# Reordering block 0's attention, one block's mask, a residual sum and the last block in a hand-ordered four-layer kernel on one Trainium2 core

## The chip, the cores and the metric

The kernel runs on one core of a Trainium2 chip. The metric is device microseconds of one execution. The engines have their own instruction queues and work in order, each by itself: TensorE (PE) multiplies, VectorE (DVE), ScalarE (ACT) and GpSimd (POOL) do the elementwise work, SyncE (SP) issues most DMAs. They meet only through semaphores.

## The reference, cut to what matters

Four layers, each added to its input, on x of 128 rows x 32 tokens x 128 features. The third and the fourth choose weights by row.

```python
def _L0_cond_ref(hidden, W1, b1, v, prompt_type_ids):      # pooling with a per-row mask
    scores = jnp.einsum('bsa,a->bs', jnp.tanh(jnp.einsum('bsd,da->bsa', hidden, W1) + b1), v)
    p = jax.nn.softmax(jnp.where(mask, scores[:, None, :], NEG_INF), axis=-1)
    return jnp.einsum('bjl,bld->bjd', p, hidden) / cnt[..., None]
...
def _L1_cond_ref(...):                                     # attention, 16 heads of 8
    dense_out = jnp.einsum('bhqk,bhkd->bhqd', jax.nn.softmax(scores + bias, axis=-1), V)
    ...
    return out @ Wo.T + bo
def _L2_cond_ref(...):                                     # 512 hidden units, low-rank experts
    hidden_i = jnp.einsum('bsd,fd->bsf', x, wi)
    hidden_i += ALPHA * jnp.einsum('bsr,fr->bsf', jnp.einsum('bsd,rd->bsr', x, common_wi_a), common_wi_b)
    hidden_i = jax.nn.relu(hidden_i + _expert_lora(x, expert_ids, experts_wi_a, experts_wi_b))
    ...                                                    # the same pattern with wo, back to 128
def _L3_cond_ref(...):                                     # 512 units, 32 of 128 outputs by expert
    h = jax.nn.gelu(jnp.einsum('bnd,hd->bnh', x, fc1_w) + fc1_b, approximate=False)
    shared = jnp.einsum('bnh,sh->bns', h, fc2_w) + fc2_b
    expert_x = jnp.einsum('bnh,bph->bnp', h, experts_w[indices]) + experts_b[indices][:, None, :]
x = x + _L0_cond_ref(...); x = x + _L1_cond_ref(...); x = x + _L2_cond_ref(...); x = x + _L3_cond_ref(...)
```

## The kernel before

The 4096 tokens are cut into 8 blocks (`NBLK`) of 512 tokens, 16 rows each. Features lie on partitions. There is no scheduler: each engine's program is written out by hand, and what stands in it first runs first. Each engine has three parts.

**Preparation and block 0.** Weights are folded while they arrive. The second projection of layer 2 is folded per expert: `base_out` and `pairs_out` (PE, L821, L834) build it in four PSUM banks for each half, and `expert_out` (ACT, L528) copies it to `weff`. In between runs block 0's attention, in four groups of heads: `scores` (PE, L714), `score_max` (DVE, L1161, L1166), `subtract_max` (POOL, L382), `exps` (ACT, L507), `turn` (DVE, L1172), `weigh` (PE, L729), `normalise` (DVE, L1178, L1181). `pool_weights` (DVE, L1117 to L1136) with `l0_exps` and `spread_weights` (ACT) is the first layer's softmax for the next block. `weight_lows` (POOL, L419) and `weight_highs` (ACT) split weights into two parts. `keep_busy` (PE, L643) multiplies into a bank that nobody reads.

**Steps 1 to 7** (`step_of(n, last)`; 2 to 6 are a loop). A step holds attention of block n, layer 2 of block n-1, the second half of layer 3 of block n-2 (`last`), and pooling of block n+1. `low` and `mask_low` make the low-rank input of `hidden_expert`; `hidden` and `hidden_expert` fill a bank (list `HID`), `relu` empties it; `out_rows` (PE, L786) multiplies by the row's own weights `rwo`. Those weights are gathered from `weff`: SP copies 12 of a block's 16 rows by DMA (`gather`, L277; `DMA_ROWS`), POOL 4 (`out_weights`, L413). At the end of a step `out_turn` (PE, L793) turns layer 2's output, `x3` (DVE, L1215, L1216, L1219) adds it and splits the sum into a high part, the sum and a low part; `x2` (DVE, L1191) is the attention's sum for block n, which ACT's `x2_high` (L534) and DVE's `x2_low` (L1195) split; `fc1` (PE, L846 to L850 and one chunk more) needs the high part of x3 for its first six matmuls and then the low part; the next step's `low` (PE, L739 to L743) needs both parts of x2.

**The end.** After step 7 come layer 2 of block 7, `final` of block 6 (PE, L869), and layer 3 of block 7. POOL's `expert_weights` (L403) writes block 7's expert weights over block 6's, 4 rows as soon as one part of `final` of block 6 has read them (`row_ps`), and then `biased_x3` (L390); PE's `token_major(7)` (L859) waits for that sum, and `final_by_chunk` (L887) for all 16 rows.

Of the kernel before, what the change touches and what calls it, by code (L numbers as in the profile page):

```python
# [25 lines left out]
P = 128  # L26
# [3 lines left out]
Q4 = P // S  # L30
# [37 lines left out]
EARLY = W_END + R_END + I_END  # L68
DMA_ROWS = [r for r in range(ROWS) if r % Q4 != Q4 - 1]


def cond_resid_kernel(nc, xt, xn, ints, bools, cols, attn_w, rank_w, ffn_w, fc2t, e3t, out):
    with ExitStack() as ctx:
# [100 lines left out]
        pS = [pS0, pS1]  # L174
        GIN = [pB1, pB2, pS0, pS1]
# [62 lines left out]
        def _(sp):  # L238
# [32 lines left out]
            def gather(i):  # L271

                for r in DMA_ROWS:
# [9 lines left out]
            gather(0)  # L283
# [15 lines left out]
        def _(pool):  # L299
# [115 lines left out]

            def weight_lows(to, first, width, n):

                at(pool, w_high, n)
                pool.tensor_tensor(ffn_p[1][:, to:to + width], ffn_s[:, first:first + width],  # L419
                                   ffn_p[0][:, to:to + width], ALU.subtract).then_inc(w_low, 1)  # L420
# [10 lines left out]
                               emask[:, :].unsqueeze(2).to_broadcast([P, 2, D]), ALU.mult).then_inc(bpair_sb, 1)  # L431
            later_ids()
            weight_lows(N_EIA, W_EIA, P + F, 1)
            subtract_max(0, 2)
            weight_lows(N_FC1, W_FC1, F, 2)
            subtract_max(0, 3)
            weight_lows(N_I, W_I, F, 3)

            def step_of(n):
# [9 lines left out]
                subtract_max(n, 1)  # L449
                expert_weights(n - 1, 0)  # L450
# [17 lines left out]
        def _(act):  # L468
# [40 lines left out]
            def relu(i, c):  # L509
                at(act, hid_ps, FC * i + c + 1)  # L510
                act.activation(hid[:, c, :], [pB1, pB2, pB0, pB1][c][:, :], ACT.Relu).then_inc(hid_sb, 1)  # L511
# [61 lines left out]
            exps(0, 0)  # L573
            weight_highs(N_FC1, W_FC1, F)
            exps(0, 1)
            out_factor()
            tanh(1)
            exps(0, 2)
            l0_exps(1)
            expert_out(0, 0)  # L580
            expert_out(0, 1)
            exps(0, 3)
            expert_out(0, 2)
            expert_out(0, 3)
            spread_weights(1)
            act.wait_ge(prep, P_PRODUCTS)
            weight_highs(N_I, W_I, F)
# [39 lines left out]
            for c in range(FC):  # L627
                relu(NBLK - 1, c)
# [9 lines left out]
        def _(pe):  # L638
# [115 lines left out]
            HID = [pB1, pB2, pB0, pB1]  # L754
# [6 lines left out]
            def hidden(i, c):  # L761

                if c == 1:
# [6 lines left out]
                parts3(HID[c][:, :], weight(N_I, c), whole(x2p), True, False)  # L770

            def hidden_expert(i, c):

                at(pe, low_sb, 2 * (i + 1))
                parts3(HID[c][:, :], weight(N_EIB, c), whole(lowp), False, True, (lowl_sb, i + 1)).then_inc(hid_ps, 1)
# [153 lines left out]
            keep_busy(3, pS0, x2p[0])  # L929
# [16 lines left out]
            base_out(0, 2)
            base_out(0, 3)
            pairs_out(0)
            weigh(0, 1)
            base_out(1, 0)  # L950
            base_out(1, 1)
            weigh(0, 2)
# [8 lines left out]
            def step_of(n, last, next_block=True):  # L961
# [31 lines left out]
                hidden_expert(n - 1, 0)  # L993
                scores(n, 1)
                hidden(n - 1, 1)
# [22 lines left out]
            low(NBLK - 1)  # L1018
            final(NBLK - 2, 0, pA0)
            final(NBLK - 2, 1, pA0)  # L1020
            for c in range(FC):
                hidden(NBLK - 1, c)
                hidden_expert(NBLK - 1, c)
            final(NBLK - 2, 2, pA0)
            out_rows(NBLK - 1, *range(G))
# [10 lines left out]
        def _(dve):  # L1036
# [176 lines left out]
            def x3(i):  # L1213
                at(dve, outT_ps, i + 1)
                tt(x3p[0][:, :], pB0[:, :], x2T[:, :], ALU.add).then_inc(x3h_sb, 1)  # L1215
                tt(x3T[:, :], pB0[:, :], x2T[:, :], ALU.add).then_inc(x3_sb, 1)  # L1216
                at(dve, x3_sb, i + 1)
# [44 lines left out]
            pool_weights(1, 0)  # L1262
            turn(0, 2)
            normalise(0, 0)
# [145 lines left out]
```

## Time and profile before

| | us |
|---|---|
| median of 3 runs (lowest, highest) | 259.78 (258.68, 262.64) |
| the profiled execution's own time | 258.46 |
| its span from first to last instruction | 256.7 |
| PE busy | 245.5 (96%) |
| DVE, ACT, POOL busy | 187.5, 137.7, 121.7 |

The span is what the trace covers; 1.8 us lie around it. A busy PE says nothing on where a single stage waits, so the stages are read one by one: 0 to 39.3 us is the preparation with block 0, 39.3 to 67.1 step 1, then six steps to 231 us, and the end to 256.7.

### The profile page before, as it was taken

How to read it: one execution, taken by the hardware profiler on the slowest of the kernel's cores; microseconds unless marked ns; L12 is line 12 of the kernel's file. 1: busy time of each engine (PE TensorE's matmuls, PEld its weight loads, DVE VectorE, ACT ScalarE, POOL GpSimd, SP SyncE). 2: the span in 40 equal slices, each digit the busy share in tenths (PEclk: the TensorE clock that was granted, in tenths of full speed). 3: DMA queues.
4: the chain of work that ended last, by engine and by line, in shares of the span. 5: the costliest groups of instructions: out<-in, count | busy, mean ns of one | idle time of the engine just before them, and what ended most of it. 6: DMA issues, size and time to landing. Idle time of an engine off the chain costs nothing.

```text
span 256.7 us, 12675 instructions
## 1 busy us (share of the span) xinstructions
PE 245.5 (96%) x4862; PEld 183.9 (72%) x4862; DVE 187.5 (73%) x349; ACT 137.7 (54%) x253; POOL 121.7 (47%) x242
## 2 busy tenths in 40 slices
PE   7999999897999999999999999999999999889993
PEld 5666455676687858787778767786878587758983
DVE  4879887886878787887888787878787868563041
ACT  3175455672819653774648382858196528541250
POOL 5876612653515461645345443536154445464240
PEclk9999999999999999999999999999999999999999
DMA  6978403550455225530654055503554541255011
GB/s 182 369 238 244 137 3 125 222 208 31 127 206 208 86 76 213 204 123 6 239 204 163 0 200 200 214 0 132 200 205 189 211 169 43 84 222 193 3 43 43
DMA packets 27326, 38.27 MB, mean 149 GB/s; under 512 B 10769, under 2 KB 11537, under 8 KB 27170
## 3 DMA queue, kind: packets, MB, share of 16 engines
q1 hardware_dynamic: 26578, 36.99, 40.3%
q10 hardware_dynamic: 720, 0.89, 1.2%
q8 instruction: 20, 0.33, 0.5%
q14 instruction: 8, 0.07, 0.1%
HBM read 10.60 MB, written 2.10 MB: 49 GB/s over the span
## 4 chain that ended last, share of the span: by engine, by line
PE 82%; SPq 5%; DVE 5%; DMA 3%; ACT 2%; issue 2%; ACTq 0%; DVEq 0%
PE pB L786 11%; PE pB L869 9%; PE pB L739 7%; PE pB L743 6%; PE pooled L714 6%; PE pB L740 6%; PE pooled L682 5%; PE pV L729 4%; PE pooled L676 3%; PE pV L694 3%; SPq L277 2%; PE pV L735 2%; SPq L276 2%; PE pB L846 2%; PE pB L821 2%
## 5 line engine op out<-in xcount | busy, mean ns | idle before, releaser
L403 POOL COPY rw<-e3t_s 128x128 f32 x128 | 40.5, 317 | 54.6 <-issue 50.0
L382 POOL TENSOR_TENSOR sc<-sc,rmax 128x512 f32<-128x512 f32 x32 | 33.7, 1052 | 42.5 <-DVE rmax L1166 42.4
L507 ACT ACTIVATE ex<-sc 128x512 f32<-128x512 f32 x32 | 20.2, 630 | 27.3 <-POOL sc L382 26.9
L786 PE MATMUL pB<-rwo,hid 128*32 128x128 f32 x1024 | 33.3, 275 | 1.4 <-DMA rwo<-weff 1.3
L786 PEld LDWEIGHTS pB<-rwo,hid 128*32 128x32 f32 x1024 | 26.7, 109 | 5.1 <-issue 2.6
L1161 DVE SCALAR_TENSOR_TENSOR sc<-pooled,bias 128x512 f32<-128x512 f32 x32 | 21.7, 678 | 11.6 <-PE pooled L714 9.7
L413 POOL COPY rwo<-weff 128x512 f32 x32 | 21.4, 674 | 16.9 <-ACT weff L528 5.8
L1172 DVE STREAM_TRANSPOSE pt<-ex 128x512 f32<-128x512 f32 x32 | 22.4, 700 | 6.5 <-ACT ex L507 6.5
L511 ACT ACTIVATE hid<-pB 128x512 f32<-128x512 f32 x32 | 18.3, 594 | 12.0 <-PE pB L743 11.7
L869 PE MATMUL pB<-rw,hT 128*32 128x128 f32 x768 | 24.4, 274 | 0.0
L1166 DVE TENSOR_REDUCE rmax<-sc 128x16 f32<-128x512 f32 x32 | 22.0, 686 | 1.1
L500 ACT ACTIVATE vb<-pV 32x512 f32<-32x512 f32 x32 | 20.1, 627 | 4.0 <-PE pV L694 3.4
L869 PEld LDWEIGHTS pB<-rw,hT 128*32 128x32 f32 x768 | 20.3, 110 | 2.0 <-issue 1.4
L534 ACT ACTIVATE x_h<-x2T 128x512 fp32r<-128x512 f32 x8 | 5.1, 633 | 28.0 <-DVE x2T L1191 28.0
L1151 DVE SCALAR_TENSOR_TENSOR kb<-pooled,bqk,cols_s 128x2048 f32<-128x2048 f32 x8 | 18.7, 2343 | 1.8 <-PE pooled L682 1.8
L714 PE MATMUL pooled<-kb,qT 32*32 32x128 f32 x1024 | 18.4, 272 | 1.4 <-DVE sc L1161 1.3
L1215 DVE TENSOR_TENSOR x_h<-pB,x2T 128x512 fp32r<-128x512 f32 x8 | 5.5, 692 | 18.6 <-PE pB L793 18.6
L714 PEld LDWEIGHTS pooled<-kb,qT 32*32 32x32 f32 x1024 | 14.2, 103 | 6.1 <-issue 6.1
L739 PE MATMUL pB<-x_h,ffn_h 128*128 128x512 f32 x40 | 18.3, 457 | 0.0
L743 PE MATMUL pB<-x_l,ffn_h 128*128 128x512 f32 x40 | 16.5, 413 | 0.5 <-DVE x_l L1195 0.5
L539 ACT ACT_TABLE_LOAD x13 | 16.7, 1283 | 0.2
L729 PEld LDWEIGHTS pV<-vb,pt 128*32 128x32 f32 x1024 | 12.4, 110 | 5.0 <-issue 2.7
(181 smaller groups left out, 521.1 us busy)
## 6 DMA issues: line engine op xcount, KB each, us to landing
rwo<-weff SPq DMA_DIRECT2D x96, 256.0 KB, 2.3
rw<-fc2t_dram SPq DMA_DIRECT2D x4, 768.0 KB, 12.3
xT<-xt_dram SPq DMA_DIRECT2D x7, 256.0 KB, 2.7
xN<-xn_dram SPq DMA_DIRECT2D x7, 256.0 KB, 2.9
out_dram<-o_s SPq DMA_DIRECT2D x7, 256.0 KB, 2.3
e3t_s<-e3t_dram SPq DMA_DIRECT2D x1, 1024.0 KB, 10.5
rwo<-ffn_w_dram SPq DMA_DIRECT2D x1, 896.0 KB, 6.4
rwo<-ffn_w_dram SPq DMA_DIRECT2D x1, 512.0 KB, 12.0
```

Of the source, the lines that this page charges most:

```text
L382: pool.tensor_tensor(sc[:, g % 2, :, :], sc[:, g % 2, :, :], rmax[:, g % 2, :].unsqueeze(2).to_broadcast([P, H, S]), ALU.subtract).then_in ...
L403: pool.tensor_copy(rw[:, r, :, SHARED:D], e3t_s[:, bass.ds(e, 1), :, :].rearrange("p o c n -> p (o c) n"))\
L413: pool.tensor_copy(rwo[:, row, :, :].rearrange("p c d -> p (c d)"), weff[:, bass.ds(e, 1), :, :].rearrange("p o c d -> p (o c d)")).then_i ...
L714: last[u] = mm(by_head(pS[u])[S * q:S * q + S, :, g, :], qT[k, row], kb[k, :, row], start=True, stop=True)
L729: last = mm(pV[S * h4:S * h4 + S, at_col:at_col + w], pt[:, hg % 2, G * h4 + g, :], vb[:, g, H4 * hg + h4, :, :], start=True, stop=True)
L739: mm(ps, w[0], x[0], start=start, stop=False)
L743: return mm(ps, w[0], x[1], start=False, stop=stop)
L786: last = mm(pB2[S * q:S * q + S, P * g:P * g + P], hid[:, c, tok], rwo[:, Q4 * g + q, c, :], start=(c == 0), stop=(c == FC - 1))
L869: last = mm(ps[S * q:S * q + S, P * g:P * g + P], hT[:, c, tok], rw[:, Q4 * g + q, c, :], start=(c == 0), stop=(c == FC - 1))
L1161: stt(sc[:, g % 2, :, :].rearrange("p (h g) t -> p h (g t)", h=H4), pS[g % 2][:, :].rearrange("p (h t) -> p h t", h=H4), SCALE, bias[:, ba ...
L1166: dve.tensor_reduce(rmax[:, g % 2, :], sc[:, g % 2, :, :], AX.X, ALU.max).then_inc(mx_sb, 1)
L1172: dve.transpose(pt[:, g % 2, :, :], ex[:, g % 2, :, :]).then_inc(pt_sb, 1)
```

## The change

Five edits, all but two of them pure order.

- **Block 0.** PE: three `keep_busy` fewer before the first scores, three more taken out later (13 become 7 in this part); the next block's `scorer_in` and `weigh` come earlier, `weigh(0, 1)` and `weigh(0, 2)` ahead of `pairs_out(0)` and of `base_out(1, ...)`. ACT: `exps` ahead of `expert_out` and weight copies. POOL: `subtract_max(0, 2)` and `(0, 3)` ahead of index and weight work. DVE: `pool_weights(1, 0)` behind `turn(0, 2)` and `normalise(0, 0)`.
- **Step 1.** DVE's `mask_low(0)` stands behind both `score_max(1, 0)` and `(1, 1)`; PE's `hidden_expert(0, 0)` behind `scores(1, 1)`.
- **One row more by POOL.** Row 14 of block 0 (`POOL_ROW`) is copied by POOL behind `subtract_max(1, 1)`; SP gathers 11 rows for that block.
- **x2 sooner.** In every step `x2` stands between the first two and the last operation of `x3`.
- **Other end.** `hidden(7, 1)` fills another bank (`HID_END`) and stands ahead of `final` of block 6; `final(6, 2)` and `final(6, 3)` stand behind `out_rows(7)` and `out_turn(7)`; two `keep_busy` are gone.

```diff
+POOL_ROW = ROWS - 2
+        HID_END = [pB1, pA1, pB0, pB1]
 # SP
-            gather(0)
+            gather(0, [r for r in DMA_ROWS if r != POOL_ROW])
 # POOL
+            def one_more_row(i):
+                e = pool.value_load(e2i[0:1, bass.ds(ROWS * i + POOL_ROW, 1)], min_val=0, max_val=E2 - 1)
+                pool.tensor_copy(rwo[:, POOL_ROW, :, :].rearrange("p c d -> p (c d)"),
+                                 weff[:, bass.ds(e, 1), :, :].rearrange("p o c d -> p (o c d)"))\
+                    .then_inc(rwo_sb[POOL_ROW // Q4], 16)
+            subtract_max(0, 2)
+            weight_lows(N_EIA, W_EIA, P + F, 1)
+            subtract_max(0, 3)
             later_ids()
-            weight_lows(N_EIA, W_EIA, P + F, 1)
-            subtract_max(0, 2)
             weight_lows(N_FC1, W_FC1, F, 2)
-            subtract_max(0, 3)
 # DVE, a step
-                x3(n - 1)
+                x3_high(n - 1)
                 x2(n)
+                x3_low(n - 1)
 # DVE, x2
                 at(dve, wo_ps, i + 1)
+                at(dve, x3_sb, i)
 # PE, the end
             low(NBLK - 1)
+            hidden(NBLK - 1, 1, HID_END)
             final(NBLK - 2, 0, pA0)
             final(NBLK - 2, 1, pA0)
...
-            final(NBLK - 2, 2, pA0)
             out_rows(NBLK - 1, *range(G))
+            final(NBLK - 2, 2, pA0)
+            out_turn(NBLK - 1)
             final(NBLK - 2, 3, pA0)
-            out_turn(NBLK - 1)
             token_major(NBLK - 2, pA1)
-            keep_busy(2, pS0, ffn_p[0])
             fc1(NBLK - 1)
```

DVE in the preparation, from the third group's turn on. `pt` is `turn`, `rc` and `on` are `normalise`, `l0s` and `l0m` are `pool_weights(1, 0)`. Before:

```order
L1117 SCALAR_TENSOR_TENSOR l0s<-masked,pooled 128x128
L1120 TENSOR_REDUCE l0m<-l0s 128x4
L1122 TENSOR_TENSOR l0s<-l0s,l0m 128x128
L1172 STREAM_TRANSPOSE pt<-ex 128x512
L1178 RECIPROCAL rc<-pV 128x32
L1181 TENSOR_TENSOR on<-pV,rc 128x16x8 x2
```

The same place after:

```order
L1191 STREAM_TRANSPOSE pt<-ex 128x512
L1197 RECIPROCAL rc<-pV 128x32
L1200 TENSOR_TENSOR on<-pV,rc 128x16x8 x2
L1136 SCALAR_TENSOR_TENSOR l0s<-masked,pooled 128x128
L1139 TENSOR_REDUCE l0m<-l0s 128x4
L1141 TENSOR_TENSOR l0s<-l0s,l0m 128x128
```

The three `pool_weights` operations now stand behind the turn and a normalisation, which waits for PE's second `weigh`.

PE at the end, from the last expert chunk of layer 2 on: `pB2<-rwo,hid` is `out_rows(7)`, `pooled<-rw,hT` is `final` of block 6, `pB0<-cols_s,lowm` is `out_turn(7)`, `pooled<-cols_s,x3bn` is `token_major(6)`. Before:

```order
L869 MATMUL pooled<-rw,hT 32x128 x16
L786 MATMUL pB2<-rwo,hid 32x128 x64
L869 MATMUL pooled<-rw,hT 32x128 x16
L793 MATMUL pB0<-cols_s,lowm 128x128 x4
L859 MATMUL pooled<-cols_s,x3bn 128x128 x4
L643 MATMUL pooled<-ffn_h 128x512 x2
```

The same place after:

```order
L797 MATMUL pB2<-rwo,hid 32x128 x64
L880 MATMUL pooled<-rw,hT 32x128 x16
L804 MATMUL pB0<-cols_s,lowm 128x128 x4
L880 MATMUL pooled<-rw,hT 32x128 x16
L870 MATMUL pooled<-cols_s,x3bn 128x128 x4
```

Both parts of `final` moved back, one behind `out_rows(7)`, one behind `out_turn(7)`.

## Rows read from the trace of the kernel before

**Rows 1.** The chain that ended last, share of the span by engine.

```profile
PE 82%; SPq 5%; DVE 5%; DMA 3%; ACT 2%; issue 2%; ACTq 0%; DVEq 0%
```

**Rows 2.** Stretches: us, busy us of PE, PEld, DVE, ACT, POOL; granted clock; DMA.

```profile
12.00:39.30 27.30, 26.51 (x374) 15.61 (x370) 23.38 (x47) 15.48 (x28) 15.04 (x22) 1.00 0.53 157
39.30:67.10 27.80, 25.02 (x470) 18.54 (x467) 21.31 (x41) 15.45 (x31) 13.23 (x26) 1.00 0.38 135
94.40:121.60 27.20, 27.20 (x592) 20.94 (x591) 22.11 (x41) 16.37 (x32) 12.78 (x26) 1.00 0.38 145
```

**Rows 3.** Timeline of DVE, tail of step 2: start, us, instruction.

```profile
91.28 0.69 DVE L1219 TENSOR_TENSOR x_l<-x3T,x_h 128x512 fp32r<-128x512 f32 x1
91.89 0.74 DVE L1191 SCALAR_TENSOR_TENSOR x2T<-pV,bo_eff,x1T 128x512 f32<-128x512 f32 x1
```

**Rows 4.** Timeline of PE, the same tail.

```profile
92.19 0.63 PE L850 MATMUL pB<-x_l,ffn_h 128*128 128x512 f32 x2
...
94.08 0.50 PE L743 MATMUL pB<-x_l,ffn_h 128*128 128x512 f32 x1
94.42 1.88 PE L682 MATMUL pooled<-x1T,attn_s 128*128 128x512 f32 x4
```

**Rows 5.** Timeline of PE, the end; in brackets idle before and releaser.

```profile
230.01 0.50 PE L743 MATMUL pB<-x_l,ffn_h 128*128 128x512 f32 x1 [0.48 <-DVE x_l L1195]
231.06 1.96 PE L869 MATMUL pooled<-rw,hT 128*32 128x128 f32 x64 [0.55 <-ACT hT L515]
...
238.65 1.08 PE L869 MATMUL pooled<-rw,hT 128*32 128x128 f32 x32
239.54 3.68 PE L786 MATMUL pB<-rwo,hid 128*32 128x128 f32 x128
...
248.34 0.60 PE L859 MATMUL pB<-cols_s,x3bn 128*128 128x128 f32 x4
```

**Rows 6.** Timeline of ACT (last relu) and of POOL, the end.

```profile
238.75 0.60 ACT L511 ACTIVATE hid<-pB 128x512 f32<-128x512 f32 x1 [0.76 <-PE pB L743]
...
240.48 0.30 POOL L403 COPY rw<-e3t_s 128x128 f32 x1 [1.82 <-PE pooled L869]
241.15 0.30 POOL L403 COPY rw<-e3t_s 128x128 f32 x1 [0.37 <-issue]
...
244.85 0.30 POOL L403 COPY rw<-e3t_s 128x128 f32 x1 [2.07 <-PE pooled L869]
...
247.10 1.05 POOL L390 TENSOR_TENSOR x3bn<-x3T,fbias 128x512 f32<-128x512 f32 x1
```

**Rows 7.** Timeline of SP's queue and of PE, step 1.

```profile
42.49 14.36 SPq L277 DMA_DIRECT2D rwo<-weff  x12
...
60.01 1.08 PE L786 MATMUL pB<-rwo,hid 128*32 128x128 f32 x32 [1.31 <-DMA rwo<-weff]
```

**Rows 8.** The chain of waits in step 1, start and us.

```profile
56.37 3.60 DMA rwo<-weff
```

**Rows 9.** Timeline of PE, the preparation.

```profile
17.14 0.94 PE L643 MATMUL pooled<-x_h 128*128 128x512 f32 x3
...
29.59 0.48 PE L834 MATMUL pB<-rwo 32*128 32x256 f32 x1
...
30.67 0.47 PE L729 MATMUL pV<-vb,pt 128*32 128x36 f32 x32
31.41 1.12 PE L821 MATMUL pB<-rwo,cols_s 128*128 128x512 f32 x2 [0.27 <-ACT weff L528]
```

**Rows 10.** Timeline of ACT, DVE and POOL, the preparation, and one DVE row of step 2.

```profile
30.76 0.60 ACT L528 ACTIVATE weff<-pB 128x512 f32<-128x512 f32 x1 [0.59 <-PE pB L834]
...
28.69 1.13 DVE L1122 TENSOR_TENSOR l0s<-l0s,l0m 128x128 f32<-128x128 f32 x1
...
100.08 0.29 DVE L1122 TENSOR_TENSOR l0s<-l0s,l0m 128x128 f32<-128x128 f32 x1
...
28.62 1.06 POOL L382 TENSOR_TENSOR sc<-sc,rmax 128x512 f32<-128x512 f32 x1
```

More of the change, by code:

```diff
@@ L269, in _, with gather @@
             load_x(2)
-            def gather(i):
-                for r in DMA_ROWS:
+            def gather(i, rows=DMA_ROWS):
+                for r in rows:
                     if r % Q4 == 0:
@@ L449, in step_of @@
                 subtract_max(n, 1)
+                if isinstance(n, int) and n == 1:
+                    one_more_row(0)
                 expert_weights(n - 1, 0)
@@ L573, in _ @@
             exps(0, 0)
+            tanh(1)
+            exps(0, 1)
             weight_highs(N_FC1, W_FC1, F)
-            exps(0, 1)
             out_factor()
-            tanh(1)
             exps(0, 2)
+            act.wait_ge(prep, P_PRODUCTS)
+            weight_highs(N_I, W_I, F)
+            exps(0, 3)
             l0_exps(1)
@@ L581, in _ @@
             expert_out(0, 1)
-            exps(0, 3)
             expert_out(0, 2)
+            spread_weights(1)
             expert_out(0, 3)
-            spread_weights(1)
-            act.wait_ge(prep, P_PRODUCTS)
-            weight_highs(N_I, W_I, F)
             x2_high(0)
@@ L627, in _ @@
             for c in range(FC):
-                relu(NBLK - 1, c)
+                relu(NBLK - 1, c, HID_END)
             out_rows(NBLK - 1)
@@ L759, in low, with hidden @@
                 parts3(pB0[:, :], weight(N_EIA), whole(x2p), True, True, (x2l_sb, i + 1)).then_inc(low_ps, 1)
-            def hidden(i, c):
-                if c == 1:
+            def hidden(i, c, banks=HID):
+                if c == 1 and banks is HID:
                     at(pe, res_sb, i - 1 if isinstance(i, int) and i == NBLK - 1 else i)
@@ L947, in _ @@
             base_out(0, 3)
+            weigh(0, 1)
             pairs_out(0)
-            weigh(0, 1)
+            weigh(0, 2)
             base_out(1, 0)
             base_out(1, 1)
-            weigh(0, 2)
             weigh(0, 3)
@@ L992, in step_of @@
                 hidden(n - 1, 0)
-                hidden_expert(n - 1, 0)
+                if last is None:
+                    hidden(n - 1, 1)
+                else:
+                    hidden_expert(n - 1, 0)
                 scores(n, 1)
-                hidden(n - 1, 1)
+                if last is None:
+                    hidden_expert(n - 1, 0)
+                else:
+                    hidden(n - 1, 1)
                 hidden_expert(n - 1, 1)
@@ L1018, in _ @@
             low(NBLK - 1)
+            hidden(NBLK - 1, 1, HID_END)
             final(NBLK - 2, 0, pA0)
             final(NBLK - 2, 1, pA0)
-            for c in range(FC):
+            hidden(NBLK - 1, 0)
+            hidden_expert(NBLK - 1, 0)
+            hidden_expert(NBLK - 1, 1, HID_END)
+            for c in range(2, FC):
                 hidden(NBLK - 1, c)
                 hidden_expert(NBLK - 1, c)
+            out_rows(NBLK - 1, *range(G))
             final(NBLK - 2, 2, pA0)
-            out_rows(NBLK - 1, *range(G))
+            out_turn(NBLK - 1)
             final(NBLK - 2, 3, pA0)
-            out_turn(NBLK - 1)
             token_major(NBLK - 2, pA1)
-            keep_busy(2, pS0, ffn_p[0])
             fc1(NBLK - 1)
@@ L1261, in _ @@
             score_max(0, 3)
-            pool_weights(1, 0)
             turn(0, 2)
             normalise(0, 0)
+            pool_weights(1, 0)
+            turn(0, 3)
             pool_weights(1, 1)
-            turn(0, 3)
             normalise(0, 1)
@@ L1285, in step_of @@
                 score_max(n, 1)
+                if last is None:
+                    dve.wait_ge(ids_sb, IDS_END)
+                    mask_low(n - 1)
                 if last is not None:
```

36 lines of the change are left out of this document (17 added, 19 removed).

## The prediction

> **What bounds the kernel now.** I read the chain that ended last first: 82% of it is PE [rows 1]. Such a share is a mean over stages, so the table of stretches came next [rows 2]. In a loop step PE is busy for 27.20 of 27.20 us: what lengthens PE's own queue there lengthens the kernel by as much, six times over, and what shortens a wait of another engine is worth nothing. The preparation leaves 0.8 us of 27.3 idle, step 1 leaves 2.8 of 27.8: only there can waits be taken away, some 3.6 us together. Then I read the timelines at the four places that the change touches, and asked of each which wait ends last. The granted clock is 1.00 (2.4 GHz) in every stretch shown, so the clock has no part in the sum.
>
> **x2 sooner (steps 1 to 6).** `x3`'s last operation, the low part, starts at 91.28 and ends at 91.97; `x2` follows with 0.74 us [rows 3]. PE's first multiplication that needs the low part begins at 92.19 [rows 4], so the old order has 0.22 us in hand. In the new order `x2` takes the low part's place: it starts at 91.28, ends about 92.02, and the low part (0.69, overlapping the one before it by 0.08, as the two rows do now) ends at 92.63. PE now arrives first. It has done its six multiplications by the high part and stands until about 92.69, half a microsecond later than now. From there to the next step's projections, which begin at 94.42, there are nine multiplications; the last of them, `low`'s third, already waits a little for x2's low part (its row is 0.50 long and the next engine row starts 0.34 behind it, where the usual distance is 0.23). That little wait goes, because `x2_low` comes no later than now: I give back 0.05 of the 0.50 for it. Net +0.45 us a step. Nothing behind it can absorb this, since PE has no idle time in a step [rows 2]. ACT's `x2_high` comes 0.6 sooner, but the GELUs behind it need the same delayed multiplications. Steps 1 to 6 have this tail: 6 x 0.45 = **+2.7 us**. Step 7's tail is counted with the end.
>
> **Other end.** Two holes of PE lie ahead of `final(6, 0)`: 0.48 us in `low(7)` and 0.55 us before the GELUs are done [rows 5]. `hidden(7, 1)`, three multiplications of 0.23, now fills the second. The low part of x3 costs its half microsecond here as well, but takes it out of the first hole, since x2 comes sooner. `final(6, 0)` starts near 231.0 as before, with 0.7 us of work behind it that stood ahead: layer 2's last chunk ends at about 237.9 in place of 238.65 [rows 5]. Then order decides. Now `final(6, 2)` hides the last relu (238.75 to 239.35 [rows 6]); without that cover `out_rows(7)`, three quarters of a group in, waits about 0.35. `out_rows` takes 3.5 (239.54 to 243.04 as the next begins; its row is 3.68 long with the drain) [rows 5], and `final(6, 2)` about 1.05 more: it ends at 237.9 + 0.35 + 3.5 + 1.05 = 242.8, where it used to end at 239.73 (238.65 + 1.08).
>
> POOL hangs on that. Its part 2 of `expert_weights` started 0.75 us behind that end (240.48), its part 3 waited 2.07 us for `final(6, 3)`, and `biased_x3` closes the row at 248.15; PE's `token_major(7)` begins 0.2 later, at 248.34 [rows 5, 6]. So POOL was just in time, and all of its eight copies now stand behind 242.8. They come 0.67 apart (240.48 to 241.15 [rows 6]), 0.30 each: 242.8 + 0.75 + 7 x 0.67 + 0.30 = 248.55. `biased_x3` adds 1.05: 249.6. `final(6, 3)`, now behind `out_turn`, is over by then, and PE itself, with its two `keep_busy` gone, would be at `token_major(7)` near 247.5. It waits about 2 us for POOL and goes on at about 249.65: 1.3 later than 248.34. Bounds: -0.85, if POOL were no bound (0.7 + 0.5 for the `keep_busy` less 0.35 for the relu), to +1.7, if the part boundary costs POOL 0.3 more. I take **+1.3**, since these durations are POOL's own rows in the same place.
>
> **Block 0.** Six `keep_busy` are gone at about 0.3 each (three in 0.94 [rows 9]): 1.8 us. The first scores come 0.8 sooner, and DVE, POOL and ACT, which wait for them in turn, follow. The question is what is late next. `base_out(1, 0)` needs a bank that `expert_out(0, 0)` empties: it waited 0.27 at 31.41 for ACT's row at 30.76 [rows 9, 10]. In ACT's new program only `l0_exps(1)` still stands between the last `exps` and that copy, and it needs DVE's three `pool_weights` operations. These now stand behind `normalise(0, 0)`, so behind `weigh(0, 1)`. That `weigh` began at 30.67; six `keep_busy` (1.8) and `pairs_out(0)` (29.59 to 30.67, 1.1) [rows 9] are no longer ahead of it, so 27.8, and 28.3 when done. `normalise` and two small operations take 1.5: at 29.8 comes the subtraction, at 0.29 or more, then the 0.3 of `l0_exps`.
>
> What the subtraction costs is the unknown. Before, it took 1.13 us, and ended with a POOL operation that had begun 0.07 us ahead of it; in a step with POOL idle it takes 0.29 [rows 10]. In the new order POOL is then in `weight_lows`, which was moved behind the two `subtract_max`. The Trainium skill ("SBUF — State Buffer", section "SBUF: two separate sides") gives a rule for this: an operation of VectorE with two SBUF inputs and one of GpSimd share a pair of ports, and the one that starts second waits for the whole of the other; the trace agrees, with 1.13 against 0.29. By that rule the subtraction again ends with POOL's operation, and `expert_out(0, 0)` starts at 31.2; without it at 30.4. I take 31.2, the row nearest to it being the 1.13: 0.45 later than 30.76. Behind it PE has 0.65 less to do than before (`weigh(0, 2)`, 0.47 [rows 9], and a short wait that followed it). So the preparation ends 0.2 sooner; bounds: 0.5 later (if the 0.65 doesn't come back) to 1.05 sooner.
>
> **Step 1: one row fewer by SP, masks later.** `out_rows(0, 3)` waited 1.31 us for the last gathered row, to 60.01 [rows 7]. SP's twelve issues fill 14.36 us, 1.2 each [rows 7]; the last, at 56.37, landed 3.60 later [rows 8]. With eleven, and 0.2 from the preparation, that row lands 1.4 sooner, at 58.6. The work that covers the rest is PE's own: it would arrive at about 58.1 by its queue, as it came 1.31 ahead of 60.01 (58.7) and the prep's 0.2 and some of the 1.25 us that it stood ahead of `scores(1, 1)` come off. DVE's mask, now behind both `score_max`, gives that wait up, but `hidden_expert(0, 0)` then waits for the mask itself, and the exponentials of step 1 still wait for ACT's values, which nothing moves: I cost it at nothing in either direction, from -0.5 to +0.5. POOL's row costs it about 0.9 us (a copy and its index) between `subtract_max(1, 1)` and the expert copies; `subtract_max(1, 2)` stands behind that, and the scores' lead covers it. So preparation and step 1 together: **-1.5 us**, bounds -2.5 and -0.5.
>
> **Sum.** The profiled execution took 258.46 us (span 256.7 and 1.8 around it). 258.46 - 1.5 + 2.7 + 1.3 = 260.96. The three timed runs lie 0.2, 1.3 and 4.2 above that execution, so their median, 259.78, is a little high against it; I predict **261.0**, under a percent from no change. About 2% (5.2 us) is what a measurement of this kernel can tell from no change.
>
> **Rivals.**
> - *The low part of x3 isn't what fc1 waits for*: then the loop is unchanged. For it: today no PE row waits there. Against: only 0.22 us of margin for a shift of 0.66 [rows 3, 4]. 260.96 - 2.7 = 258.3. Chance 0.12.
> - *POOL doesn't set the end*: 260.96 - 1.3 - 0.85 = 258.8. For it: POOL's copies are 0.30 each with 0.37 of issue between, which might shrink. Against: the same distance in every copy of the end [rows 6]. Chance 0.13. Both together: 256.1, chance 0.06.
> - *Slower: x3's low part is blocked by POOL.* It too has two SBUF inputs, and now starts 0.6 later, while POOL is copying expert rows (0.30 each, 0.67 to 0.75 apart). If it starts within such a copy, it waits for the rest of it. It decides from the moment that a copy is running at 91.9 in the step's own time; price up to 0.30 a step, 1.8 in six: 262.8. Against: the copies fill less than half of the time. Chance 0.10.
> - *The new order of block 0 gives all that it takes out* (1.05 in place of 0.2, step 1 following with the SP start): 260.1, inside the forecast's own range. The forecast, with this: 0.55. Left over, 0.04.
>
> The range takes in all but the case of both rivals and the far ends: 257.8 to 263.3. Faster by over 2% needs all three losses to be absent and more: 0.03. Slower by over 2% needs the fourth case with every bound against: 0.03. Within: 0.94.
>
> **What the new profile would show.** Right: in each loop step PE stands about 0.5 us before the multiplications by x3's low part, and a step takes 27.6 in place of 27.2; `token_major(7)` begins behind a wait of about 2 us for POOL's `biased_x3`; `out_rows(0, 3)` begins near 58.5; `base_out(1, 0)` begins behind a wait of over a microsecond for `weff`. Wrong: loop steps of 27.2 us or less; an end in which PE goes straight from `fc1(7)` into `token_major(7)`; a gather that lands as late as 60; or a stretch with a granted clock under 1.00 behind one of the two new holes, which no row here prices.

## The result, and the profile after

| | before | after |
|---|---|---|
| median, us (lowest, highest; runs) | 259.23 (258.39, 262.64; 4) | 264.5 (264.03, 264.92; 4) |
| ratio, 95% interval | | 1.0225 [1.018, 1.0269] |
| profiled execution, span, us | 258.46, 256.7 | 264.6, 262.8 |
| mean granted clock of the profiled execution | 1.000 | 0.981 |

The changed kernel is about 2.3% slower (1.8 to 2.7%): 264.5 against the 261.0 that was predicted, and above the range (257.8 to 263.3). Ratios here and below leave out executions more than 1.5% above the fastest of their kernel; medians and extremes are over all executions, and where TensorE's clock fell in some of them the text counts these.

I cut both spans at the first query projection of each step (PE, L682 before, L694 after) and took the differences.

| stretch | before | after | difference |
|---|---|---|---|
| preparation and block 0, from 13.03 | 26.23 | 29.92 | +3.69 |
| step 1 | 27.86 | 27.50 | -0.36 |
| steps 2 to 6 together | 136.33 | 138.52 | +2.19 |
| step 7 and the end | 53.25 | 53.83 | +0.58 |

The sum, 6.1, is the difference of the spans. The first line is the surprise. Two lines of the page of the changed kernel, the granted clock in 40 slices and the chain that ended last ([rows 1] of before), say where to look:

```profile
PEclk9995799999999999999999999999999999999999
...
PE 81%; DVE 10%; issue 4%; POOLq 2%; DMA 2%; ACT 1%; POOL 0%; ACTq 0%; DVEq 0%
```

The clock has a dip in the fourth and fifth slice, 20 to 33 us. In the chain DVE's share has doubled, 5% to 10%: PE now stands for DVE in every step. The stretches of the changed kernel that answer to [rows 2] (us; busy us of PE, PEld, DVE, ACT, POOL; granted clock; DMA share, GB/s):

```profile
12.00:43.00 31.00, 29.46 (x368) 17.19 (x364) 22.24 (x47) 15.24 (x28) 15.04 (x22) 0.83 0.47 136
43.00:70.60 27.60, 25.59 (x470) 18.61 (x468) 22.07 (x41) 16.04 (x32) 13.96 (x27) 1.00 0.37 129
98.36:126.05 27.69, 27.28 (x593) 20.98 (x592) 22.58 (x41) 16.40 (x32) 12.83 (x26) 1.00 0.38 142
```

The preparation has six multiplications fewer (368 records against 374), yet PE is busy 2.95 us longer: the same work at a mean granted clock of 0.83 in place of 1.00. A loop step now has 0.41 us without PE, where it had none. Finer stretches of the changed kernel's preparation:

```profile
18.00:19.00 1.00, 1.00 (x29) 0.57 (x13) 0.67 (x2) 0.98 (x2) 0.19 (x1) 1.00 0.17 46
19.00:20.00 1.00, 1.00 (x3) 0.50 (x2) 0.97 (x3) 0.95 (x3) 0.04 (x1) 0.60 0.25 71
20.00:22.00 2.00, 2.00 (x12) 0.86 (x10) 1.84 (x4) 1.80 (x3) 1.73 (x2) 0.50 1.02 275
...
26.00:28.00 2.00, 2.00 (x5) 0.77 (x4) 1.86 (x6) 0.00 (x0) 1.11 (x2) 0.50 1.13 308
...
29.00:30.00 1.00, 1.00 (x34) 0.79 (x34) 0.93 (x2) 0.95 (x2) 0.44 (x1) 0.78 0.02 4
30.00:32.00 2.00, 2.00 (x7) 0.98 (x6) 0.71 (x1) 1.31 (x3) 1.89 (x3) 1.00 0.02 4
```

From 19.2 to 29.4 us, 10.2 us, the granted clock is 0.50, the 1.2 GHz level. PE's busy share is 1.00 ahead of the fall, at it and through all of these ten microseconds. From 13.03 us on PE has no wait ahead of it, and it is none of the places named in the prediction. Timeline of the changed kernel: PE in the preparation, at `out_rows(0, 3)`, in step 1's tail and at the end; DVE in the preparation and in step 1's tail; POOL at the end; SP's queue (start, us, instruction; in brackets the idle time before and its releaser):

```profile
17.20 1.15 PE L726 MATMUL pooled<-kb,qT 32*32 32x128 f32 x64
18.29 0.96 PE L655 MATMUL pooled<-x_h 128*128 128x512 f32 x3
19.18 2.07 PE L908 MATMUL pB<-rwo 16*128 16x512 f32 x2
...
35.79 1.13 PE L832 MATMUL pB<-rwo,cols_s 128*128 128x512 f32 x2 [1.21 <-ACT weff L540]
...
62.12 0.64 PE L797 MATMUL pB<-rwo,hid 128*32 128x128 f32 x16
63.26 0.65 PE L797 MATMUL pB<-rwo,hid 128*32 128x128 f32 x16 [0.49 <-issue]
...
68.27 0.72 PE L861 MATMUL pB<-x_l,ffn_h 128*128 128x512 f32 x2 [0.40 <-DVE x_l L1241]
...
255.43 0.66 PE L870 MATMUL pB<-cols_s,x3bn 128*128 128x128 f32 x4 [1.99 <-POOL x3bn L393]
...
34.51 0.39 DVE L1141 TENSOR_TENSOR l0s<-l0s,l0m 128x128 f32<-128x128 f32 x1
...
66.87 0.75 DVE L1211 SCALAR_TENSOR_TENSOR x2T<-pV,bo_eff,x1T 128x512 f32<-128x512 f32 x1
67.53 0.68 DVE L1241 TENSOR_TENSOR x_l<-x3T,x_h 128x512 fp32r<-128x512 f32 x1
...
249.26 0.29 POOL L406 COPY rw<-e3t_s 128x128 f32 x1 [4.85 <-PE pooled L880]
...
254.33 1.04 POOL L393 TENSOR_TENSOR x3bn<-x3T,fbias 128x512 f32<-128x512 f32 x1
...
46.18 12.89 SPq L280 DMA_DIRECT2D rwo<-weff  x11
...
259.45 1.76 SPq L297 DMA_DIRECT2D out_dram<-o_s  x4
```

Five things are to be seen.

- The clock: before, three `keep_busy` ran from 17.14, ahead of the first scores [rows 9]. Now the scores start at 17.20, three `keep_busy` follow, and in the next real work, two multiplications of 512 columns by 16 rows, the clock falls: 2.07 us for the two.
- x2 sooner: `x2` stands ahead of the low part, as it should, and PE stands 0.40 before its first multiplication by it. In [rows 4] there is no such wait.
- The end: `token_major(7)` waits 1.99 for POOL's `biased_x3`. It begins 46.46 after step 7's start; it was 44.89 [rows 5].
- Step 1: SP's eleven issues take 12.89 where twelve took 14.36 [rows 7]. `out_rows(0, 3)` no longer waits for a gathered row. It begins at 62.12, 19.17 behind the step's start (before: 20.75); in place of the 1.31 there are 0.49, halfway through its 32 multiplications, that no event of the profile explains.
- `base_out(1, 0)` waits 1.21 for `weff`, as predicted, though late, at 35.79.

### The profile page after: what moved, and what is told of

It reads as the page before. It is cut to its first block, busy times and chain, and to the rows that moved or that the text cites. A ratio compares the mean times of both kernels' runs of the same rounds, so it can differ in the third digit from the quotient of the medians.

```text
span 262.8 us, 12666 instructions
## 1 busy us (share of the span) xinstructions
PE 248.5 (95%) x4854; PEld 184.9 (70%) x4854; DVE 189.3 (72%) x349; ACT 138.1 (53%) x253; POOL 122.2 (46%) x243
## 4 chain that ended last, share of the span: by engine, by line
PE 81%; DVE 10%; issue 4%; POOLq 2%; DMA 2%; ACT 1%; POOL 0%; ACTq 0%; DVEq 0%
PE pB L797 12%; PE pB L880 9%; PE pB L751 7%; PE pooled L726 7%; PE pB L755 6%; PE pB L752 6%; PE pooled L694 5%; PE pV L741 4%; PE pV L706 3%; PE pooled L688 3%; PE pB L832 2%; PE pB L861 2%; DVE x_l L1241 2%; DVE x_h L1235 2%; DVE x3T L1236 2%
## 5 line engine op out<-in xcount | busy, mean ns | idle before, releaser
L416 POOL COPY rwo<-weff 128x512 f32 x32 | 20.1, 628 | 24.3 <-ACT weff L540 11.4
L726 PE MATMUL pooled<-kb,qT 32*32 32x128 f32 x1024 | 19.3, 281 | 0.3 <-issue 0.2
L726 PEld LDWEIGHTS pooled<-kb,qT 32*32 32x32 f32 x1024 | 14.9, 107 | 4.9 <-issue 4.9
L751 PE MATMUL pB<-x_h,ffn_h 128*128 128x512 f32 x39 | 17.7, 455 | 0.0
L694 PE MATMUL pooled<-x1T,attn_s 128*128 128x512 f32 x32 | 15.2, 598 | 0.3 <-DVE x1T L1165 0.3
```

The costliest lines, as they stand in the source:

```text
L416: pool.tensor_copy(rwo[:, row, :, :].rearrange("p c d -> p (c d)"), weff[:, bass.ds(e, 1), :, :].rearrange("p o c d -> p (o c d)")).then_i ...
L694: mm(ps[:, :], w[:, :], x1T[:, :], start=True, stop=True).then_inc(done, 1)
L726: last[u] = mm(by_head(pS[u])[S * q:S * q + S, :, g, :], qT[k, row], kb[k, :, row], start=True, stop=True)
L751: mm(ps, w[0], x[0], start=start, stop=False)
```

## The experiments

Theory A, in the expectations: the `keep_busy` ahead of the first scores held the granted clock, and what they cost in time was less than what they kept. The rival has the time in the new order itself, in its holes and waits. Twelve kernels were timed, and the kernel before beside them, with medians of 258.57 (8 executions, beside e1 to e4), 258.66 (25, e5 to e8) and 258.64 (35, e9 to e12). A fall of the size seen above takes some 0.019 off an execution's mean granted clock (10.2 us at half of 262.8), so I count executions with a mean of 0.987 or less. Where in such an execution the clock fell is known only for the profiled ones, and two of the shorter falls of 3.4 us that e1 and e4 show come to 0.987 as well.

### e1: the changed kernel with three keep_busy put back

```diff
             prepare_wo()
+            keep_busy(3, pS0, x2p[0])
             scores(0, 0)
```

> The changed kernel with the three multiplications ahead of the first scores put back, all else as changed. Theory A (the granted clock fell at 19.4 us because these three are gone, and that alone made the preparation 3.7 us longer): the granted clock is 1.00 throughout, the projections of step 1 begin at 39 to 39.5 us in place of 42.95, the time is 260.3 to 261.3, 3.3 to 4.2 under the changed kernel. Rival B (the new order of block 0 itself costs it, or lets the clock fall later): the clock still falls or the preparation still ends beyond 41 us, time 263 or more.

Measured: 264.87 us (263.88 to 265.65), ratio 1.0239 [1.0199, 1.028]. The preparation takes 28.21. Timeline (PE, DVE, POOL), then stretches, of this kernel:

```profile
32.47 1.37 PE L832 MATMUL pB<-rwo,cols_s 128*128 128x512 f32 x2 [1.88 <-ACT weff L540]
...
253.80 0.66 PE L870 MATMUL pB<-cols_s,x3bn 128*128 128x128 f32 x4 [1.99 <-POOL x3bn L393]
...
30.52 1.06 DVE L1142 TENSOR_TENSOR l0s<-l0s,l0m 128x128 f32<-128x128 f32 x1
...
30.17 2.55 POOL L429 TENSOR_TENSOR ffn_l<-rwo,ffn_h 128x512 fp32r<-128x512 f32 x2
```

```profile
32.00:33.00 1.00, 0.53 (x1) 0.30 (x2) 0.90 (x5) 1.00 (x3) 0.72 (x1) 1.00 0.00 0
33.00:34.00 1.00, 1.00 (x3) 0.53 (x2) 0.58 (x2) 0.71 (x3) 0.00 (x0) 0.61 0.00 0
34.00:36.00 2.00, 2.00 (x34) 0.53 (x32) 0.00 (x0) 1.51 (x4) 0.00 (x0) 0.50 0.00 0
...
256.00:257.00 1.00, 1.00 (x28) 1.00 (x24) 0.00 (x0) 0.00 (x0) 0.00 (x0) 0.50 0.00 0
```

The fall at 19 us is gone: the clock stays at 1.00 up to 33.2. So far A holds. But the kernel is no faster, and A's time of 260.3 to 261.3 is missed: the clock now falls behind another place, the 1.88 us for which PE waits before `base_out(1, 0)`, from 33.2 to 36.6. It falls once more at the end, behind the wait for POOL, from 255.1 to 258.5, and the end takes 56.32. The changed kernel has two holes behind which the clock can fall, and the early fall had covered the first: with PE slowed, the wait there was only 1.21. The prediction's arithmetic of that hole is borne out by the subtraction: begun 0.35 us into the first of POOL's two operations, it takes 1.06, as in the row of 1.13 [rows 10]; in the changed kernel, where it begins near the end of POOL's pair, it is over in 0.39. This agrees with the rule that the prediction takes from the Trainium skill ("SBUF — State Buffer", section "SBUF: two separate sides").

### e2: the kernel before without those three

```diff
             prepare_wo()
-            keep_busy(3, pS0, x2p[0])
             scores(0, 0)
```

> The kernel before with only the three multiplications ahead of the first scores taken out. Theory A: the clock falls to half near 19.4 us and comes back near 29, the preparation ends some 3.5 us later, time 262 to 264. Rival B: the clock stays at 1.00 and the time is that of the kernel before within 1 us.

Measured: 261.82 us (260.51 to 263.41), ratio 1.0137 [1.0082, 1.0193]; mean clocks 0.977, 0.976, 0.987, 0.974. Stretches of this kernel:

```profile
18.00:19.00 1.00, 1.00 (x17) 0.48 (x3) 0.69 (x1) 0.97 (x2) 0.03 (x1) 1.00 0.05 20
19.00:20.00 1.00, 1.00 (x3) 0.47 (x3) 0.97 (x2) 0.95 (x3) 0.20 (x1) 0.59 0.07 25
20.00:21.00 1.00, 1.00 (x4) 0.48 (x2) 0.97 (x3) 0.97 (x2) 0.84 (x1) 0.50 0.57 143
```

This one deletion gives the whole of it: the fall comes at the same microsecond, 19.2, and lasts to 29.4, the preparation takes 30.11 in place of 26.23, and steps and end are as before. Nothing else was changed, so taking away 0.9 us of work made the preparation 3.9 longer. The early fall needs nothing of block 0's new order.

### e3: x2 sooner alone

```diff
-                x3(n - 1)
+                x3_high(n - 1)
                 x2(n)
+                x3_low(n - 1)
```

> The kernel before with only x2 moved between the two parts of x3. The prediction's step: TensorE waits 0.4 to 0.5 us for x3's low part in each of steps 1 to 7, a loop step takes 27.7 in place of 27.27, time 2.4 to 3.0 above the kernel before. Rival: another part of the change made the loop steps longer, then a step stays at 27.3 and the time within 0.5.

Measured: 261.89 us (261.26 to 262.93), ratio 1.0145 [1.0107, 1.0183]; mean clocks 0.999, 0.993, 1.00, 0.990. The medians lie 3.3 apart; the two executions with a clock near 1.00 took 261.38 and 261.26, 2.7 to 2.8 above the median of before. Steps 3 to 6 take 27.70 in place of a mean of 27.27, step 2 takes 28.03, with PE standing 0.48 before the low part. This part of the sum is as predicted: 0.43 a step, 0.50 with step 2.

### e4: the other end alone

`HID_END`, the order of `final` and the loss of the two `keep_busy` at the end, all else as before.

> The kernel before with only the other end. The prediction's step: the last token-major turn waits about 2 us for GpSimd's sum and begins 1.3 us later, time 1.0 to 1.7 above the kernel before. Rival (the trace of the changed kernel, where from the last x3 of step 7 to the end of the span only 0.3 us more were taken, is the rule): the stores at the very end take that back, time 0 to 0.5 above.

Measured: 262.54 us (260.32 to 264.8; 5 runs), ratio 1.0123 [1.0053, 1.0192]. The end takes 56.25. Timeline of PE, then stretches, of this kernel:

```profile
48.56 1.14 PE L716 MATMUL pooled<-kb,qT 32*32 32x128 f32 x64 [1.26 <-DVE sc L1164]
...
250.72 0.66 PE L859 MATMUL pB<-cols_s,x3bn 128*128 128x128 f32 x4 [1.99 <-POOL x3bn L392]
```

```profile
51.00:53.00 2.00, 2.00 (x6) 1.54 (x6) 1.94 (x4) 1.15 (x2) 1.16 (x4) 0.50 0.64 235
...
252.00:254.00 2.00, 2.00 (x45) 2.00 (x41) 0.00 (x0) 0.07 (x1) 0.00 (x0) 0.50 0.00 0
```

The wait for POOL is there, 1.99 as predicted. Behind it the clock fell for 3.4 us in this execution, which the prediction had not priced. It also fell in step 1, from 50.5 to 53.9, behind the wait of 1.26 before the second scores; this kernel and the one before have the same step 1, so that hole may do it in the kernel before too. Of its 68 executions 22 have a mean of 0.988 to 0.994, about the size of one such fall (3.4 us at half of 257 take off 0.007), but where it fell in them is not known. By the medians e4 is 4.0 slower, beyond the 1.0 to 1.7 expected. The one execution with a clock of 1.00 took 260.32, some 1.7 more than the median of before: the end without the fall.

### e5: e1 with the hole of the preparation filled

```diff
             weigh(0, 2)
+            keep_busy(10, pS1, x2p[0])
             base_out(1, 0)
```

> Run e1's kernel with ten more keep-busy multiplications in the hole of block 0 (between the third weighing and the base product that waits for ACT). Theory A (e1's preparation was 2.0 us longer because the hole of 1.9 us let the clock fall at 33.4): with the hole filled the clock stays at 1.00 to the end of the preparation, the projections of step 1 begin at 39.0 to 40.2 in place of 41.09, the time is 0.8 to 2 under e1. Rival B (the waits of the new order, not the clock, make the 2.0): the projections begin at 41 or later and the time is e1's.

Measured: 263.2 us (261.96 to 264.47; 4 runs), ratio 1.0207 [1.0143, 1.0271]. Timeline of PE of this kernel:

```profile
30.34 2.57 PE L655 MATMUL pooled<-x_h 128*128 128x512 f32 x10
32.75 1.02 PE L832 MATMUL pB<-rwo,cols_s 128*128 128x512 f32 x2
```

In the profiled execution the clock is 1.00 from end to end and the preparation takes 27.10, where e1 took 28.21. That is the order of block 0 with its clock held: 0.87 more than before, of which 0.8 are the three multiplications put back and up to 0.46 is filling beyond the hole's length (`base_out` begins 20.05 behind the first projection, 19.59 in e1, and no wait is left before it). Two executions at 1.00 took 262.38 and 261.96; less the 0.8, this is 261.2 to 261.6, inside the forecast's range; the other two, at 0.993 and 0.994, took 264.0 and 264.5. So what the forecast's total missed is the clock and little else.

### e6: e4 with the wait for POOL filled

```diff
             fc1(NBLK - 1)
+            keep_busy(8, pV, ffn_p[0])
             token_major(NBLK - 1, pB0)
```

> Run e4's kernel (only the other end) with eight keep-busy multiplications between the last fc1 and the last token-major turn, which waits for GpSimd. Theory A (the wait for GpSimd costs 1.3 us, and behind that hole the clock falls, which makes the last product twice as long: the other 2 us or so of e4's end of 56.25 against 53.25): the clock stays at 1.00 to the end, the end is 54.2 to 55, the time 1 to 2 us under e4. Rival B (the clock has no part in it): the end stays at 56.

Measured: 259.59 us (258.7 to 264.54; 10 runs), ratio 1.0036 [1.0002, 1.0071]. Timeline of PE of this kernel:

```profile
249.94 0.66 PE L859 MATMUL pB<-cols_s,x3bn 128*128 128x128 f32 x4 [0.17 <-POOL x3bn L392]
```

The end takes 54.18, 0.93 more than before, against 3.0 more in e4. `keep_busy` costs nothing where PE would stand anyway (`token_major(7)` begins 46.12 behind step 7's start, 46.17 in e4), and against e4's execution, in which the clock fell, it gave back 2 us. The clock doesn't always fall there: in e5 the wait is 1.99, not filled, and the clock held.

### e7: one row more by POOL and masks later, on the kernel before

The three edits of step 1 in the change (row 14, `mask_low(0)` behind both `score_max`, `hidden_expert(0, 0)` behind `scores(1, 1)`), nothing else.

> The kernel before with only the one row more by GpSimd and step 1's masks later. The prediction's step: the last gathered row lands 1.2 us sooner, step 1 is 1.0 to 1.5 us shorter than 27.86, the time 0.8 to 1.6 under the kernel before. Rival: the mask's own wait gives it back, step 1 at 27.5 or more, time within 0.5 of the kernel before.

Measured: 257.42 us (257.18 to 262.67; 11 runs), ratio 0.9956 [0.9929, 0.9983]. Seven executions lie at 257.2 to 257.4 with clocks of 0.998 to 1.00; in four the clock fell (mean 0.976 to 0.98; 261.1 to 262.7), though all three `keep_busy` are in place. The profiled one is one of the four. Its stretches, then PE's timeline in step 1:

```profile
18.00:19.00 1.00, 1.00 (x65) 0.80 (x50) 0.00 (x0) 0.95 (x3) 0.00 (x0) 0.99 0.06 25
19.00:20.00 1.00, 1.00 (x3) 0.60 (x3) 0.94 (x2) 0.98 (x2) 0.00 (x0) 0.50 0.07 24
```

```profile
51.67 1.15 PE L724 MATMUL pooled<-kb,qT 32*32 32x128 f32 x64
53.57 0.50 PE L749 MATMUL pB<-lowp_h,ffn_h 128*128 128x512 f32 x1 [0.74 <-DVE lowp_h L1225]
```

Step 1 takes 27.14, 0.7 less than before: the wait of 1.26 ahead of `scores(1, 1)` is gone, and 0.74 before `hidden_expert(0, 0)` have taken its place. The step was expected to gain 1.0 to 1.5; it is short of that. And the fall at 19 us isn't the changed kernel's alone: here it runs from 19.0 to 29.2 with the three multiplications in place. It is a matter of chance there, and the three multiplications make it rarer.

### e8: the fill at the end alone

`hidden(7, 1)` into its other bank ahead of `final(6, 0)`, while `final(6, 2)`, `final(6, 3)` and the two `keep_busy` stand as before.

> The kernel before with one part of the other end alone: hidden(7, 1) in its other bank fills the hole ahead of final of block 6, and both later parts of final and the two keep-busy stay where they were. By the prediction's terms: 0.5 to 0.8 us gained ahead of the outputs, GpSimd's copies come as much sooner, time 0.4 to 0.9 under the kernel before, clock at 1.00. Rival: GpSimd's sum or the stores at the end take it back, time within 0.3.

Measured: 257.8 us (256.63 to 258.64; 10 runs), ratio 0.9983 [0.9961, 1.0004]; the profiled end takes 51.98, 1.27 less than before. Timeline of PE of this kernel:

```profile
247.11 0.60 PE L859 MATMUL pB<-cols_s,x3bn 128*128 128x128 f32 x4
```

No wait for POOL. So of the other end the fill gains, and it is the move of the two parts of `final` behind `out_rows(7)` and `out_turn(7)` that makes POOL late. Of the 1.27, 0.60 are an earlier `token_major(7)` (44.29 behind step 7's start, 44.89 before); the stores at the end, 2.16 long here and 2.75 in the kernel before, make up nearly all the rest. By the medians the gain is 0.9 us; the interval of the ratio still holds 1.

### e9: the three moved behind the first scores

```diff
-            keep_busy(3, pS0, x2p[0])
             scores(0, 0)
-            keep_busy(3, pA0, x2p[0])
+            keep_busy(6, pA0, x2p[0])
```

> The kernel before with the three multiplications moved from ahead of the first scores to behind them: as many, one place later. Theory A1 (what counts is what TensorE did before the clock is granted or not, near 19.2 us; work behind the scores comes too late): the clock falls near 19.4 as in e2, the preparation takes 29 us or more. Theory A2 (only the amount of work in the preparation counts): the clock stays at 1.00, the preparation is 26.2 or a little less, time that of the kernel before within 0.7.

Measured: 258.83 us (257.36 to 264.87; 10 runs), ratio 0.998 [0.9945, 1.0015]. The clock fell in 3 of 10 executions (means 0.968, 0.98, 0.968). In the profiled one, with 259.48, it held at 1.00 through the preparation (26.12) and fell in step 1, behind the hole of 1.26, for 3.4 us. Stretches of it:

```profile
50.00:52.00 2.00, 2.00 (x6) 1.55 (x5) 1.97 (x4) 1.23 (x2) 1.05 (x4) 0.50 0.61 220
52.00:54.00 2.00, 2.00 (x7) 1.41 (x5) 1.56 (x3) 0.89 (x2) 1.63 (x3) 0.65 0.70 263
```

Neither A1 nor A2 is borne out. With all six behind the scores 3 of 10 executions have such a mean, against 4 of 4 without three; whether the place matters stays open, for 3 of 10 is neither e2's count nor the kernel before's (3 of 35 beside it, 5 of 68 in all), and where the clock fell in these three isn't known.

### e10: the row alone

Row 14 by POOL, `mask_low(0)` and `hidden_expert(0, 0)` where they were.

> The kernel before with only the one row more by GpSimd, masks as before. If the gather alone bounds step 1: the same 27.1 that e7 showed, time 0.8 to 1.3 under the kernel before. If the masks do their part: step 1 longer than e7's by 0.3 or more, and TensorE still waits over a microsecond for the second pair of scores.

Measured: 258.76 us (258.03 to 263.51; 10 runs), ratio 0.9998 [0.9965, 1.0031]. Step 1 takes 28.22, no less than the 27.86 of before. Timeline of POOL, ACT and PE of this kernel:

```profile
53.27 2.06 POOL L383 TENSOR_TENSOR sc<-sc,rmax 128x512 f32<-128x512 f32 x2
...
54.35 0.63 ACT L517 ACTIVATE ex<-sc 128x512 f32<-128x512 f32 x1 [2.56 <-POOL sc L383]
...
48.31 1.14 PE L724 MATMUL pooled<-kb,qT 32*32 32x128 f32 x64 [1.27 <-DVE sc L1171]
...
55.61 1.08 PE L796 MATMUL pB<-rwo,hid 128*32 128x128 f32 x32 [0.89 <-ACT hid L521]
```

The wait for the gather goes, the 1.27 before the second scores stay, and nothing is gained. POOL's extra copy makes `subtract_max(1, 2)` late, ACT waits 2.56 for it, the relus stand behind that exponential in ACT's queue, and PE waits 0.89 for the last of them. The row pays only together with the masks (e7); the masks without the row were not run.

### e11: the row, the masks and the fill at the end

The kernel before with e7's and e8's edits.

> What the runs so far point to: the kernel before with the row, the masks and hidden(7, 1) in its other bank, and with block 0, x2 and the later parts of the end as before. By the sum of e7 and e8 1.9 us under the kernel before: 256.5 to 257.2 where that has 258.66. If both meet a bound at the same place: 257.4 or more.

Measured: 256.81 us (255.96 to 261.89; 12 runs), ratio 0.994 [0.9911, 0.9969], against 258.64. It is faster than both kernels: preparation 26.25, step 1 27.15, the end 52.12. In one of its 12 executions the clock fell (0.98).

### e12: e11 with six keep_busy ahead of the first scores

```diff
-            keep_busy(3, pS0, x2p[0])
+            keep_busy(6, pS0, x2p[0])
             scores(0, 0)
```

> Run e11's kernel with six in place of three multiplications ahead of the first scores. Theory A: they cost their 0.8 us where the clock holds anyway, so 0.8 above e11, and the granted clock of every execution stays at 0.99 or more. Rival (the fall near 19 us is chance and has nothing to do with them): single executions with a mean clock near 0.98 are as frequent as in e7.

Measured: 257.72 us (256.79 to 259.77; 12 runs), ratio 0.9985 [0.9955, 1.0016]. None of the 12 falls under 0.99, and the longest is 259.77 in place of 261.89; the preparation takes 26.93, 0.7 more. So far A, but the insurance costs 0.9 in the median, and e11 itself has such a fall in only 1 of 12: 0 against 1 can't tell whether the three more multiplications do anything.

The counts of executions with a mean of 0.987 or less, by `keep_busy` in the preparation:

```
three taken out ahead of the first scores     after 4 of 4, e2 4 of 4
three moved behind the first scores           e9 3 of 10
three put back, in the new order              e1 2 of 4, e5 0 of 4
as before                                     before 5 of 68, e7 4 of 11, e10 1 of 10, e11 1 of 12, e8 0 of 10, e3 0 of 4,
                                              e6 1 of 10, e4 3 of 5
three more                                    e12 0 of 12
```

In the profiled executions of e1 and e4 such a mean came from falls in other places, as shown above. One execution each of the changed kernel, e2, e4 and the kernel before has just 0.987, which two short falls would also give; the other means counted are 0.981 or less, but for three of e1 and e4 (0.983 and 0.984). The nearest comparison is e2 against the kernel before timed beside it: 4 of 4 against 0 of 8.

## Why the prediction was wrong, point by point

**What failed: block 0.** The step said that six `keep_busy` are gone, 1.8 us, and asked only what is late next; the first part said that "the clock has no part in the sum", because it was 1.00 in every stretch before. That the clock was 1.00 was the work of what the change removed. I priced multiplications into a bank that nobody reads by their time alone. The prediction did name a fall of the clock among what would make it wrong, but "behind one of the two new holes", and not in a stretch where PE is busy without a gap. e2 shows the cause: the three multiplications alone, taken from the kernel before, bring the fall to the same microsecond and 3.9 us with it.

The size works out. With the clock held, e5's preparation less the three multiplications is 26.3, so the fall costs the changed kernel 29.92 - 26.3 = 3.6 us, or up to 0.46 more if e5's filling beyond the hole is taken off too. The forecast had -0.2 for the rest of this step, a time of 26.0; 26.3 is inside its bounds, and part of the 0.3 is e5's filling. The measured execution lies 264.6 - 260.96 = 3.6 above the sum.

**x2 sooner: right.** +0.45 a step was predicted; the changed kernel gives a mean of 27.70 a step against 27.27, e3 the same in four steps of five, and PE's wait stands where it was put. Its first rival, that the low part is not what fc1 waits for, falls. The "slower" rival, POOL blocking the low part, isn't seen: the row is 0.68 long, as before.

**The other end: the wait right, the sum of the span off by luck of the last stores.** POOL makes `token_major(7)` wait 1.99 where about 2 was predicted, and it begins 1.57 later in its stretch, where I had 1.3. The span lengthens by only 0.58, because SP's four stores at the end took 1.76 us; in the kernel before they took 2.75, as its timeline of SP's queue shows:

```profile
252.30 2.75 SPq L294 DMA_DIRECT2D out_dram<-o_s  x4
```

How long they take differs from execution to execution: with the end of before 2.42 to 2.75 (e2, e3, e7), with the other end 1.76 to 2.73 (the changed kernel, e1, e4, e5, e6). SP's queue in e5:

```profile
256.92 2.06 SPq L297 DMA_DIRECT2D out_dram<-o_s  x4
```

There the end takes 54.23, 0.98 more than before; e6 has 0.93 more. Unpriced was the clock behind that wait: in e1 and e4 it fell there and the end took 3.0 more. In the profiled executions of the changed kernel and of e5 it held.

**Step 1: a gain, but by other hands.** Preparation and step 1 were to give 1.5 back, nearly all from the row, with the masks at nothing. Step 1's own gain is 0.36, or 0.8 without x2's 0.43, where 1.3 was forecast. The gathered row came as early as forecast: `out_rows(0, 3)` begins 19.17 behind the step's start, and the prediction's 58.5 means 19.4. The pause of 0.49 inside it, which no row of before could show, is as large as what is missing. e10 shows the row alone at zero, e7 shows row and masks at 0.7: it is the order of the masks that frees PE from the 1.26 before `scores(1, 1)`, and without it POOL's extra copy gives back all that the shorter gather saves. What the masks alone would gain isn't shown. What the prediction called covered ("`subtract_max(1, 2)` stands behind that, and the scores' lead covers it") is not covered unless the scores come sooner.

So the four terms, clock aside, sum to what was forecast, 2.5 over the profiled execution of before, with 0.1 for block 0, -0.4 for step 1, 2.2 for the loop and 0.6 for the end. That they meet it so closely is in part luck: the end came out 0.7 cheaper by the stores, block 0 and step 1 0.3 and 0.5 dearer. The change was slower by the 3.6 of the clock on top.

## What to carry to other kernels

Work that is there only to keep an engine busy is priced by what the granted clock does without it, not by its own time: take it out alone first, and look at the clock of the ten microseconds behind it. A change made of five edits is tried edit by edit: here two of them and half of a third (e11) are 0.6% faster than before, and the rest had hidden that. Where a move takes more than an engine's margin (0.22 us for a shift of 0.66 here), or delays what a late engine waits for (`final` ahead of `expert_weights`), the rest of the shift comes back as a wait, once for each pass.

## What the runs showed of the hardware

**A fall of the clock with a busy PE.** The granted clock went from 1.00 to 0.50 (2.4 to 1.2 GHz) while PE's busy share was 1.00 in every stretch around it, and stayed there for some ten microseconds of full busy share (19.2 to 29.4 in the changed kernel and in e2, 19.0 to 29.2 in e7). Ahead of it PE had run the 64 small score multiplications of 32 by 32 and three wide ones, and in the changed kernel and e2 it was in two with 16 rows; in e7 it was still in the three wide ones. The Trainium skill ("TensorE: Matmul & The Clock Gate", section "Part 1: The HAM clock gate") says that a monitor sets the clock by how busy TensorE has been; the busy share of these rows was 1.00 at either level, so it doesn't show what the monitor counts. What in the work ahead brings the fall, beyond the three multiplications that e2 leaves out, the runs don't tell.

**It is a matter of chance.** Of kernels with the same instructions in the preparation 0 of 10, 1 of 10, 1 of 12 and 4 of 11 executions have such a mean (e8, e10, e11, e7). Three multiplications of 0.3 us stand between 4 of 4 (e2) and 0 of 8, 5 of 68 over all executions of the kernel before.

**Holes of 1.26 to 2 us can cost more than their length.** Behind PE's waits of 1.26 (e4, e9), 1.88 (e1) and 1.99 (e1, e4) the clock fell for 3.4 us; behind the same 1.99 in the profiled executions of the changed kernel and e5 it held, and behind the 1.25 in that of the kernel before. With the 1.88 and the 1.99 filled (e5, e6) it held in the profiled executions.

**A pause that no wait explains.** In `out_rows(0, 3)` PE pauses 0.49 us in the changed kernel (63.26) with no event of another engine ahead of it, once the gather is no longer late. PE's timeline in e1, then in e5:

```profile
61.35 0.84 PE L797 MATMUL pB<-rwo,hid 128*32 128x128 f32 x19 [0.51 <-issue]
...
60.26 1.07 PE L797 MATMUL pB<-rwo,hid 128*32 128x128 f32 x29 [0.96 <-issue]
```

It comes behind 16 of the group's 32 multiplications in the changed kernel, behind 13 in e1, which has three `keep_busy` more ahead, and behind 3 in e5, which has thirteen more; behind 10 in e4, e7, e9, e10 and e11 (six more) and 7 in e12 (nine more). So it stands behind the same number of PE's multiplications from the start, and not at one place of the work. What PE waits for there stays open.
